# Delta-rule block, 32 sequences: the Gram matrix of the keys as xh S xh^T, and xh^T handed from the key stage to the main stage

## What is computed

```python
xn = layernorm(x, dn_g, dn_b)
q, k, v = split(xn @ gates_w + gates_b, 3)
lr = xn @ lr_w + lr_b
k = k / norm(k)                             # per token
A = tril(k @ k.T, -1) + eye(T)              # T = 512
u = solve_triangular(A, v, lower=True)
score = einsum('nsk,ntk->nst', q, k)
y = einsum('nst,ntv->nsv', score, lr * u)
x = x + y @ out_w + out_b
x = x + mlp(layernorm(x, mn_g, mn_b))       # relu, 256 wide
x = x + ffn(layernorm(x))                   # silu(gate) * up, 768 wide, integer weights
```

## Time and profile before

| | |
|---|---|
| median of 3 runs | 1722.58 us (1719.63 to 1728.41) |
| the profiled execution's own time | 1726.53 us |
| its span | 1724.8 us, 31689 instructions |
| mean granted clock of TensorE | 0.979 of full speed |
| busy: PE, DVE, ACT, POOL | 96%, 69%, 50%, 46% of the span |
| gg to and from its scratch, 640 KB each | 3.4 and 3.8 us from issue to landing (median) |
| kx to its scratch, 522 KB | 2.8 us |
| x into the key stage and into the main stage, 512 KB | 4.2 and 4.7 us |

### The profile page before, as it was taken

One profiled execution on the slowest core, in us unless ns is written; L12 is line 12 of the kernel. 1 busy time (PEld: TensorE's weight loads), 2 busy tenths in 40 slices (PEclk: granted clock), 3 DMA queues, 4 the chain that ended last, 5 costly groups with the idle time before them and its releaser, 6 DMA issues.

```text
span 1724.8 us, 31689 instructions
## 1 busy us (share of the span) xinstructions
PE 1651.0 (96%) x11298; PEld 1511.2 (88%) x11298; DVE 1185.6 (69%) x2796; ACT 855.1 (50%) x1850; POOL 796.7 (46%) x1084
## 2 busy tenths in 40 slices
PE   5999999579999999999999999999999999999997
PEld 4899999568999999999999999999999999999986
DVE  4677777236777776777777767777777666666663
ACT  3677777315444444444444444444444444444442
POOL 4456777124444444444444444444444444444441
PEclk8999999869999999999999999999999999999999
DMA  3755565511111222111111211111112111122100
GB/s 117 237 181 202 195 208 196 184 37 50 57 57 57 66 83 71 56 56 56 56 56 56 93 56 63 62 56 56 56 56 81 56 56 56 56 65 69 59 13 25
DMA packets 131700, 145.34 MB, mean 84 GB/s; under 512 B 60885, under 2 KB 113368, under 8 KB 131544
## 3 DMA queue, kind: packets, MB, share of 16 engines
q1 hardware_dynamic: 131544, 143.31, 25.6%
HBM read 82.13 MB, written 61.15 MB: 83 GB/s over the span
## 4 chain that ended last, share of the span: by engine, by line
PE 77%; DVE 2%; ACT 1%; POOL 0%; issue 0%; DMA 0%; DVEq 0%; POOLq 0%; ACTq 0%
PE ps L153 31%; PE ps L1006 20%; PE ps L1016 10%; PE ps L926 7%; PE ps L920 5%; PE ps L937 4%; DMA gg<-gg_scratch 0%; DVE bs L1421 0%; POOL sc L1443 0%; DVE hl L1285 0%; ACT sg L1128 0%; DVE hf L1280 0%; DVE z_lo L1285 0%; DVE a L1416 0%; ACT z_hi L1137 0%
## 5 line engine op out<-in xcount | busy, mean ns | idle before, releaser
L1490 POOL TENSOR_TENSOR hl<-hf,hh 128x512 fp32r<-128x512 f32 x128 | 166.8, 1303 | 258.9 <-ACT hh L1133 258.9
L1016 PE MATMUL ps<-wdT,hh 128*128 128x256 f32 x768 | 204.2, 303 | 0.8 <-ACT sg L1128 0.6
L1133 ACT ACTIVATE hh<-hf 128x512 fp32r<-128x512 f32 x192 | 120.9, 629 | 165.2 <-DVE hf L1280 165.2
L1016 PE MATMUL ps<-wdT,hl 128*128 128x256 f32 x768 | 187.1, 281 | 2.0 <-DVE hl L1285 2.0
L1280 DVE TENSOR_TENSOR hf<-ps,sg 128x512 f32<-128x512 f32 x192 | 132.5, 690 | 66.8 <-PE ps L1006 63.9
L1128 ACT ACTIVATE sg<-ps 128x512 f32<-128x512 f32 x192 | 113.7, 592 | 126.6 <-PE ps L1006 126.6
L1006 PE MATMUL ps<-xh3T_hi,wgT 128*128 128x512 f32 x384 | 155.0, 404 | 1.1 <-DVE xh3T_lo L1285 1.1
L1137 ACT ACTIVATE z_hi<-ps 128x256 fp32r<-128x256 f32 x128 | 49.0, 383 | 215.6 <-PE ps L937 215.6
L1469 POOL TENSOR_TENSOR xhm_lo<-xh,xhm_hi 128x1024 fp32r<-128x1024 f32 x32 | 76.5, 2391 | 169.9 <-DVE xhm_hi L1350 169.9
L1006 PE MATMUL ps<-xh3T_hi,wuT 128*128 128x512 f32 x384 | 152.4, 397 | 0.0
L1006 PE MATMUL ps<-xh3T_lo,wgT 128*128 128x512 f32 x384 | 152.4, 397 | 0.0
(11 more groups left out here) (219 smaller groups left out, 5574.6 us busy)
## 6 DMA issues: line engine op xcount, KB each, us to landing
gg_scratch<-gg SPq DMA_DIRECT2D x32, 640.0 KB, 3.4
gg<-gg_scratch SPq DMA_DIRECT2D x32, 640.0 KB, 3.8
kx_scratch<-kx SPq DMA_DIRECT2D x32, 522.0 KB, 2.8
kx<-kx_scratch SPq DMA_DIRECT2D x32, 522.0 KB, 3.6
xk<-in_L_attn_x_dram SPq DMA_DIRECT2D x32, 512.0 KB, 4.2
xt<-in_L_attn_x_dram SPq DMA_DIRECT2D x32, 512.0 KB, 4.7
out_dram<-ot SPq DMA_DIRECT2D x32, 512.0 KB, 2.9
low_scratch<-gg SPq DMA_DIRECT2D x128, 16.0 KB, 1.5
```

The source lines that it names most:

```text
L1016: mm = pe.matmul(ps[:, (FG, FU)[j // 2], (j % 2) * C:(j % 2 + 1) * C], part[:, h, blk(j)], wdT[:, h, :], start=(h == 0 and part is hh), st ...
L1133: act.activation(hh[:, h, :], hf[:, h % 2, :], ACT.Copy).then_inc(hh_ev[h], 1)
L1490: pool.tensor_tensor(hl[:, h, :], hf[:, h % 2, :], hh[:, h, :].bitcast(F32), ALU.subtract).then_inc(hl_ev[h], 1)
```

## The change

1. S = Wk Wk^T is formed once (folded weights; transposes, products, split). The key stage multiplies S by xh^T (12 matmuls of 512 columns), splits the result (pT, with the lr columns in front) and forms the Gram rows as xh times that. No keys, squares, power or normalization, and no transposes of keys. The Gram matrix is unnormalized: its diagonal is the squared norm.
2. The scale moves: the 32x32 triangles have a diagonal that isn't one, so the inversion begins with a reciprocal and a scaling; the main stage reads the diagonal (`load_diag`) and POOL makes scales of it (`key_scales`) for xh, its bias and lr. The last product's weights become Wk Wq^T (`wqk2`).
3. The key stage stores both halves of xh^T per sequence (1 MB, instead of kx, 522 KB); the main stage loads them. Its transposes of xh and their evictions go. ACT makes xh in the order 3, 0, 1, 2 and w of block 3 from it, so both need x.
4. x is buffered three times, xh^T three, the Gram matrix twice in the key stage; POOL makes 4 inversion steps a round, DVE 10 an iteration.
5. The first loads of the main stage (`load_first`) are issued in the key stage's last rounds, and the stage's end no longer waits for the Gram stores to land; the main stage waits for them at its first use.

```diff
+        def load_diag(sp, n, done):
+            diag = bass.AP(tensor=gg_d.tensor, offset=gg_d[n].offset + OFF, ap=[[GW + 1, P], [P, TB], [1, 1]])
+                sp.dma_start(dg[:, :].unsqueeze(2), diag).then_inc(done, 16)
+        def key_scales(pool, n, loaded_, n_loaded, made, count):
+            pool.wait_ge(loaded_, n_loaded)
+            pool.tensor_tensor(ri, dg[:, :], mhalf4[:, :], ALU.pow).then_inc(made[0], 1)
+            pool.wait_ge(made[0], count)
+            pool.tensor_tensor(r, dg[:, :], ri, ALU.mult).then_inc(made[1], 1)
+            pool.tensor_tensor(l_, scal[:, n, S_LR, :], ri, ALU.mult)
+            pool.wait_ge(made[1], count)
+            pool.tensor_tensor(s_, scal[:, n, S_S, :], r, ALU.mult)
+            pool.tensor_tensor(b_, scal[:, n, S_B, :], r, ALU.mult).then_inc(made[2], 1)
...
+            def store_xhT(sp, n):
+                for k in range(CB):
+                    sp.wait_ge(xhT_lo[k], n + 1)
+                sp.dma_start(xhT_d[n], xhTk[n % 3]...).then_inc(xhT_out[n % 3], 16)
+            def keys_sp(sp):
...
+                for n in range(NS):
+                    if n >= 2:
+                        store_gram(sp, n - 2)
+                    if n + 4 < NS:
+                        sp.wait_ge(xh_done, n + 2)
+                        load_x(sp, n + 4)
+                    if n + 1 < NS:
+                        store_xhT(sp, n + 1)
...
+                    if n == INV_LAST + 2:
+                        load_first(sp)
...
+            def pe_pT(pe, n):
+                for m in range(CB):
+                    wait(pe, pT_lo[m], n)
+                    split_matmul(pe, ps[:, P0 + m, :], s2, [(slice(None), k, slice(m * P, (m + 1) * P)) for k in range(CB)],
+                                 xhTk2[n % 3], [(slice(None), k, slice(None)) for k in range(CB)], True, True, ...)
+            def pe_gram(pe, n):
+                wait(pe, g_act, n)
+                wait(pe, g_dve, n)
...
+                row(3, 3, 0, 0, 2 + C, lambda k: pe.wait_ge(pT_lo[k], n + 1))
+                row(2, 2, 0, 0, 2 + C + P)
+                row(1, 1, 0, 0, 2 + C)
+                row(0, 0, 0, 0, 2 + P)
+                row(3, 0, 2 + P, 2 + C, C).then_inc(g_ps, 1)
+            def keys_pe(pe):
...
+                for n in range(NS):
+                    pe_pT(pe, n)
+                    if n + 1 < NS:
+                        pe_xhT(pe, n + 1)
...
+                    if n >= 1:
+                        pe_gram(pe, n - 1)
+                    prep_pe(pe, n - PREP)
+                pe_gram(pe, NS - 1)
...
                         pe_wstep(pe, i, 1)
-                        pe.wait_ge(xhm_done, i + 1)
-                        after(pe, h1_ev[1], i)
-                        after(pe, ot_ev[0], i - 1)
-                        pe_transposes(pe, (S0, FG), xh, ht_ps)
                         pe_bt(pe, i, 3)
...
+                        wait(pe, xhT_in, 16 * i)
                         pe_tokens(pe, A0, 0, xhT2, m22, y_ps[0])
...
-                        act_hi(act, xhT2[0], (S0, FG), ht_ps, ht_hi, i + 1)
...
-                        dve_lo(dve, xhT2[1], xhT2[0], (S0, FG), ht_hi, ht_ev, i + 1, (0,))
                         dve_z(dve, i, 1)
-                        dve_lo(dve, xhT2[1], xhT2[0], (S0, FG), ht_hi, ht_ev, i + 1, (1,))
...
+                    if att and i + 1 < NS:
+                        after(pool, xhm_done, i, TB)
+                        after(pool, w_ev[0], i)
+                        key_scales(pool, i + 1, dg_in, 16 * (i + 1), rho_made, i + 1)
                     if r == 0:
                         wait(pool, inv_out, 32 * m)
                         invert_start(pool, lanes, m)
...
+                    load_diag(sp, n, dg_in)
                     sp.wait_ge(gl_lo, n)
+                    grams_stored(sp, n + 1)
                     sp.dma_start(gg[:, :], gg_d[n]).then_inc(gg_in, 16)
...
-                    sp.dma_start(kx[:, :], kx_d[n]).then_inc(kx_in, 16)
                     sp.wait_ge(xb_done, n)
                     sp.dma_start(xt[:, :, :], x_v[n]).then_inc(xin, 16)
+                    sp.wait_ge(y_ps[1], n)
+                    sp.dma_start(xhT[...], xhT_d[n]).then_inc(xhT_in, 16)
```

More of the change, by code:

```diff
@@ L53, in delta_block_kernel @@
     TB, CB, HB = T // P, C // P, H // P
[L54 to L60, removed]
+    LOWER = TB * (TB - 1) // 2
+    OFF = LOWER * P
+    GCOL = {(1, 0): 0, (2, 0): P, (2, 1): 2 * P, (3, 0): 3 * P, (3, 1): 4 * P, (3, 2): 5 * P}
+    GW = OFF + TB * P
+    S_S, S_B, S_R1, S_SH, S_LR = range(5)
     NSUB = T // SUB
@@ L479, in norms @@
                          (L[5], s_, m, ALU.mult)]
-                if half == 0:
-                    pool.wait_ge(mv_done, n + 1)
-                    wait(pool, ex_done, n - 1)
-                    wait(pool, xh_done, n - 1)
-                for q in range(5 * half, 5 + 3 * half):
-                    o, a, b, op = steps[q]
+                pool.wait_ge(mv_done, n + 1)
+                for q, (o, a, b, op) in enumerate(steps):
                     pool.tensor_tensor(o, a, b, op).then_inc(lstep[q], 1)
@@ L547, in pe_xhT @@
             def pe_xhT(pe, n):
                 pe.wait_ge(xh_done, n + 1)
-                wait(pe, g_ev[2], n - 2)
+                for k in range(CB):
+                    wait(pe, xhT_lo[k], n)
                 prep_evicted(pe, n - 2 - PREP)
@@ L775, in prep_pe @@
                     mm.then_inc(vo_ps, 1)
+                if q == 5:
+                    for m in range(CB):
+                        for h in range(2):
+                            for k in range(CB):
+                                mm = pe.matmul(piece(2 * m + h), wkT[:, k, m * P:(m + 1) * P], wqT[:, k, h * P:(h + 1) * P],
+                                               start=(k == 0), stop=(k == CB - 1))
+                    mm.then_inc(qk_ps, 1)
                 if FFN_AT <= q < FFN_AT + FFN_STEPS:
@@ L1473, in pool_body @@
                     if att:
-                        for j in range(TB):
-                            after(pool, x2_ev[j], i)
-                        pool.wait_ge(kx_in, (i + 1) * 16)
-                        pool.tensor_tensor(shf[:, :], kx[:, E_SH:E_SH + TB], zero4[:, :], ALU.add).then_inc(sh_done, 1)
                         wait(pool, xin, i * 16)
```

575 lines of the change are left out of this document (286 added, 289 removed).

## The result

The changed kernel takes **1678.18 us** (median of 4 runs, 1676.37 to 1680.45) against 1722.88 of the kernel before on the same chip: a ratio of 0.9738, with a 95% interval from 0.9708 to 0.9768. That is 44.7 us less. The forecast of 1670 promised 52.6 less; the range held the time.

The account below looks back on a forecast made before the run. TensorE was taken to bound both stages. From 1726.53 us, -30.4 + 5 - 2.5 - 1.5 - 12 - 1.7 - 14.9 + 3.4 = -54.6 gave 1671.9; forecast 1670, range 1650 to 1694.

Parts of the forecast that it names:

- The key stage: 31 key rounds: TensorE's matmuls per round fall from 8.59 to 7.61 us, -30.4 us in all.
- The give-back of 5 us: Key stage's last three rounds: the main stage's first loads, 2.3 MB, cost +5 us, with engines nearly full.
- the transfer rival: Key stage: transfers set the round, which falls from 9.24 to 9.0 us only; 1690 us in total, chance 0.20.
- The start: Before the second key round: longer weight chain, but no wait for normalized keys; -2.5 us, bounds -3.5 and +3.
- my sum of cold steps: Kernel start: counting the cold steps one after another put the second key round some 2.5 us earlier.
- The tail and the hole: Key stage's end after its last round, -1.5 us; TensorE's gap before the main stage, 16.4 to 4.1 us, -12.
- Iteration 0: Main stage's first iteration: removed transposes lie on its chain at half clock, twice 0.87 us, -1.7.
- The steady main stage: 31 main iterations: 0.48 us gained each, 0.39 of the transposes' 0.87 turned into waiting for xn; -14.9 us.
- signs named for it: Main stage: among the signs of being right, TensorE's wait for xn at 0.7 to 0.8 us instead of 0.35.
- a sign of being wrong: TensorE waiting at a place that the list of waits before the change doesn't have.
- The slot's start: Main iterations 8 and 16: key scales delay GpSimd's memset, TensorE feels some 1.7 us each, +3.4.
- the inversion's extra step: Main stage, VectorE: one more step per iteration, before the a0 updates where VectorE waits for TensorE, costs nothing.

Follow-up runs that it names:

- the run with the second store: Changed kernel with each sample's halves of xh^T stored a second time, to scratch that nobody reads: 1715.51 us in one run.
- putting the clearing first: Changed kernel with GpSimd's clearing of the inversion's tile moved ahead of rows plus bias and key scales at a slot's start: 1679.01 us in one run.
- xn shared: Changed kernel with one inversion step moved out of the last place, and ScalarE forming the second half of xn beside VectorE's first: 1662.31 us, ratio 0.9642.
- w(0) earlier: Against the kernel with xn split between VectorE and ScalarE, VectorE forms only xn's first block before update w(0): 1656.57 us, ratio 0.9621.

## Why the prediction was right, and where it was not

**The key stage: right.** 31 rounds gave 31.4 against 30.4, a round's matmuls 7.55 against 7.61. The 0.65 us per round that I left standing are still there as a mean (8.22 - 7.55 = 0.67); they lie in the rounds before 203.84 us. **The give-back of 5 us was wrong**: the engines weren't nearly full. The step that failed is the division of 199 GB/s by a share of 58.0%. The share counts the time that packets take, and that isn't proportional to what they carry: it was 0.62 at 211 GB/s, 0.89 at 309 and 1.03 at 397. The first gives 340 GB/s for full engines, the second 347, and full engines carried 397. So a round had 7.55 us for transfers that need 2.29 MB / 0.390 = 5.9, and the loads fitted in. The 358 GB/s that the prediction quoted from the Trainium skill (DMA: Bandwidth & Descriptors, Specifications) were passed too in the run with the second store; the Trainium skill (HBM Reference, Specifications) says that a core that streams alone goes above that share, and that run's trace agrees with its 383 to 397. The error that made me take +5 is also the one that kept the transfer rival at a chance of 0.20.

**The start: wrong by 2.** The wait for the normalized keys left, and TensorE's wait before the second round still grew from 3.52 to 7.49 us. The trace shows a path that my sum of cold steps didn't have. The first round starts at 20.10, so S is there. What the second one waits for is VectorE's remainder of its xh^T (30.67), which stands behind the statistics of a later sample, and these wait 4.64 us for GpSimd's scales. The scales come 3.1 us later than before (27.45 for 24.36), because the statistics that they need start at 20.89 instead of 17.64, behind the split of S. Nothing was tried here.

**The tail and the hole: right** (-1.4 and -11.6 for -1.5 and -12). Of the 4.8 us left, eviction 1.1, four low stores 1.8 and the Gram store 0.4 are near the forecast; the barrier is the larger part of what is missing to them, 1.4 where I had 0.6. **Iteration 0** shows no gain; its 1.7 us drown in a start-up that differs by several us between runs of the same code.

**The steady main stage: the mechanism right, one line of the sum wrong.** 0.52 per iteration for 0.48, shown by taking the transposes out of the old kernel and by putting them back into the new one. One of the signs named for it didn't come, though: the wait for xn stayed at 0.35 instead of 0.7 to 0.8, and the rest of the waiting went to the z product (0.26). That and the down product's wait are what the prediction named as a sign of being wrong, a wait of TensorE at a place that the list didn't have. The slot's start was right in size, 1.7 per slot; putting the clearing first gave back 0.95 of the 2.2 by which such an iteration stands out. What failed is the sentence on the inversion's extra step: that it "lies before the a0 updates, where VectorE waits for TensorE: nothing". I looked for idle time on VectorE and found it. I didn't look at what GpSimd does at that moment. The term was 11 us: twelve iterations of 0.95. With 3.5 for the slots' starts it took all that the transposes had brought in those 28 iterations (28 x 0.52 = 14.6). The trace of before had a sample of it, had I read it: the same kind of operation stood there sixteen times at 0.80 to 0.98 us where its median is 0.38 (0.98 at 835.44, 0.43 for the next one, of nearly the same size), in iterations that took 41.57 like their neighbours.

The Trainium skill (SBUF — State Buffer, Who interferes with whom) states the rule: a VectorE instruction with two inputs in SBUF contends with a GpSimd instruction that reads SBUF, and the one that comes second stops until the first is done. The traces agree where GpSimd works on 512 columns. Of the inversion operations in the changed kernel's main stage 31 take over 0.8 us. Three are the scaling of 1024 columns, which takes 1.21 with nothing beside it. Each of the other 28 starts during a hl of GpSimd and ends 0.05 to 0.28 us behind its end, whether it works on 31 columns or 255: the end doesn't depend on when it started, only on hl's end and its own size. The traces don't agree where GpSimd takes a power of 128x4, which also reads SBUF and lasts 1.0 us:

```profile
827.47 1.02 POOL L228 TENSOR_TENSOR rho<-dg,mhalf 128x4 f32<-128x4 f32 x1
827.51 0.41 DVE L200 TENSOR_TENSOR tmp<-low,inv 128x240 f32<-128x240 f32 x1
```

The second operation starts 0.04 behind the first, takes its usual time and ends 0.57 before it. The same holds of all 18 inversion operations that start during this power (0.21 to 0.42 us each).

So the sum of terms was 8 us too favourable (54.6 against the spans' 46.6) as a balance: the key stage gave 6 more than forecast (5 of them the give-back), the start 2 less, iteration 0 some 2 less, and 11 were lost to the collision. That the total came within 8.2 us of 1670 is therefore luck in part: the 6 us to spare in the key stage covered half of what the collision took.

## What to carry to other kernels

Before moving a small instruction to "where the engine waits anyway", look at what the *other* engines run at that moment: an operation that reads two tiles of SBUF cost the rest of GpSimd's 512-column instruction here, whatever its size, and nothing beside GpSimd's power of four columns. Look in the trace for instructions of one kind whose durations spread (0.38 and 1.49 for the same size), and ask what ended when they ended. And price idle time by starts of matmuls, not by the wait printed before a weight load; to earn it, shorten the chain that ends in it (xn shared, w(0) earlier: 0.16 and 0.19 per iteration) rather than fill it with work (0.18 lost).

## What the runs showed that was not expected

- A VectorE operation with two tiles as inputs that starts during GpSimd's hl (128x512) ends just after it: 128x31 in 1.16 us, 128x192 in 1.49, where it takes 0.2 and 0.36 alone. One that reads PSUM and one tile isn't held: 0.69 beside hl(2) as elsewhere. Nor is one with two tiles beside GpSimd's power of 128x4: 0.41 for 128x240. And it works the other way round: where hl(0) starts during VectorE's scaling of 1024 columns, hl takes 1.54 us instead of 1.29 (at 663.01).
- The transfers carried 383 to 397 GB/s over 40 us with full engines, while a share of 0.62 to 0.89 pointed to 340 to 347. A share can't be scaled up to a ceiling.
- 0.35 us of wait before a weight load was worth 0.16 us when it was removed, on an engine that the windows show as busy 199.6 of 200 us.
- The granted clock at the main stage's start is 0.50 whether 4.8 or 16.4 us of idle time stand ahead of it, and from there the first two iterations took 83.5 to 90.0 us in kernels that are the same up to there but for single instructions.
